# A graph layer pair on one core: the memset behind each gather made 128x320, and the wait at a group's head taken out

## The reference, cut to what matters

```
h = relu(layernorm(x))
x = x + segment_sum over edges of ( h[src] @ weight[etype] )          # 16 edge types, 64x64 each
h = relu(layernorm(x))
m = relu( concat(h[src], h[dst], edge_attr) @ W1 + b1 ) @ W2 + b2
x = x + segment_sum over edges of m, by dst
```

## Time and profile before

| | |
|---|---|
| median of three runs | 4952.87 us |
| profiled execution | 4951.48 us, of which the span is 4949.3 us |
| busy: PE / PEld / DVE / ACT / POOL | 55% / 31% / 30% / 12% / 69% |
| mean granted TensorE clock | 0.69 |
| gathers in the two loops | 1533 and 1661 |
| mean of one gather | 947 and 951 ns |

### The profile page before, as it was taken

How to read it: one execution, slowest core, us unless ns; L and a number is a source line. 1 busy time by engine, 2 the same in 40 slices (tenths; PEclk the granted TensorE clock), 3 DMA queues, 4 the chain that set the end, 5 groups by cost and what they waited for, 6 DMA issues and landing times.

```text
span 4949.3 us, 40507 instructions
## 1 busy us (share of the span) xinstructions
PE 2744.9 (55%) x10310; PEld 1528.5 (31%) x10310; DVE 1470.4 (30%) x2002; ACT 582.2 (12%) x1139; POOL 3439.7 (69%) x6536
## 2 busy tenths in 40 slices
PE   2656555565565655566655454555555554555555
PEld 1434333343343333333422222222222222222222
DVE  6323222222222222222233332333233232332333
ACT  3111111111111111111110000000000000000000
POOL 7567676676776776676756676777777767767676
PEclk8777777777777767776766666666666666666666
DMA  4111111111111111111111111111111111111111
GB/s 100 21 25 25 27 25 24 24 27 24 25 27 25 25 27 25 24 27 24 25 29 29 29 29 30 29 30 31 29 31 31 29 29 30 29 30 32 28 30 26
DMA packets 391188, 144.16 MB, mean 29 GB/s; under 512 B 321650, under 2 KB 337323, under 8 KB 391163
## 3 DMA queue, kind: packets, MB, share of 16 engines
q0 software_dynamic: 106304, 109.07, 11.5%
q1 hardware_dynamic: 282245, 34.18, 4.8%
q10 hardware_dynamic: 2614, 0.62, 0.1%
HBM read 129.03 MB, written 12.83 MB: 29 GB/s over the span
## 4 chain that ended last, share of the span: by engine, by line
POOL 34%; issue 23%; another core or an unknown queue 21%; PE 12%; DVE 6%; DMA 2%; DVEq 1%; ACT 1%; POOLq 0%; ACTq 0%; SPq 0%
POOL rows L710 31%; PE ps L1462 3%; PE ps L1379 2%; PE ps L1461 2%; POOL spacer L743 2%; PE ps L1466 1%; DVE z_slot L1230 1%; DVE slots L1219 1%; DVE q_blk L1243 1%; DMA rows<-p_table,idx 1%; DVEq L1234 1%; POOL spacer L763 1%; PE ps L1386 1%; DMA rows<-h_table,idx 1%
## 5 line engine op out<-in xcount | busy, mean ns | idle before, releaser
L710 POOL DMA_INDIRECT rows<-p_table,idx x1661 | 1580.3, 951 | 728.9 <-issue 510.2
L710 POOL DMA_INDIRECT rows<-h_table,idx x1533 | 1451.9, 947 | 695.9 <-issue 417.5
L1379 PE MATMUL ps<-onehot,rows 128*64 128x256 f32 x3328 | 742.2, 570 | 500.6 <-DMA rows<-h_table,idx 407.2
L1461 PE MATMUL ps<-w_attr,attr_t 64*128 64x512 f32 x416 | 368.0, 980 | 1087.4 <-DVE q_blk L1243 753.8
L1095 DVE TENSOR_TENSOR onehot<-key,ps 128x2048 f32<-128x2048 f32 x209 | 473.9, 2278 | 532.0 <-remote 344.6
L1379 PEld LDWEIGHTS ps<-onehot,rows 128*64 128x64 f32 x3328 | 364.5, 199 | 787.4 <-issue 693.2
L1219 DVE TENSOR_TENSOR slots<-ps,rows 128x512 f32<-128x512 f32 x208 | 143.8, 692 | 1263.0 <-remote 698.4
L1386 PE MATMUL ps<-w_types,slots 128*128 128x128 f32 x3328 | 464.2, 297 | 86.6 <-issue 85.3
L1386 PEld LDWEIGHTS ps<-w_types,slots 128*128 128x128 f32 x3328 | 430.6, 209 | 163.7 <-issue 157.8
L1461 PEld LDWEIGHTS ps<-w_attr,attr_t 64*128 64x128 f32 x416 | 87.8, 262 | 1125.2 <-issue 1124.8
L1462 PE MATMUL ps<-q_blk,onehot 128*128 128x512 f32 x416 | 405.9, 1077 | 0.0
(11 more groups left out here) (142 smaller groups left out, 1939.3 us busy)
## 6 DMA issues: line engine op xcount, KB each, us to landing
rows<-p_table,idx POOLq DMA_INDIRECT x1661
rows<-h_table,idx POOLq DMA_INDIRECT x1533
attr<-in_edge_attr_dram SPq DMA_DIRECT2D x52, 128.0 KB
q_win<-q_table SPq DMA_DIRECT2D x208, 32.0 KB
p_table<-pq_out SPq DMA_DIRECT2D x25, 120.0 KB
q_table<-pq_out SPq DMA_DIRECT2D x25, 120.0 KB
out_dram<-xs SPq DMA_DIRECT2D x25, 120.0 KB
xs<-in_x_dram SPq DMA_DIRECT2D x6, 480.0 KB, 6.3
```

The costliest lines, as they stand in the source:

```text
L710: pool.indirect_dma_start(rows[:, u, t, :], None, table, bass.IndirectOffsetOnAxis(ap=at, axis=0)).then_inc(s, 16)
L1379: last = pe.matmul(slot_ps[t % 2 * D:(t % 2 + 1) * D, b, t // 2, :], rows[:, u, t, :], onehot[:, b, t, :], start=True, stop=True)
L1461: pe.matmul(pre_ps[:, u % 2, :], attr_t[half, u // 2, :], w_attr[half].rearrange("k j d -> k (j d)"), start=True, stop=False)
```

## The change

The memset behind a gather writes 128 partitions by 320 columns in place of one cell. All of them write the same cells, so each waits for the one before it (`spaced`), which was issued one gather earlier. The wait for the group before at a group's head goes, in both loops. The other waits at the head stay. The counter `spaced` starts at 1 in place of 8.

```diff
-        spacer = sb("spacer", [1, T], fp32)
+        spacer = sb("spacer", [P, 5 * D], fp32)
...
+            def space(n):
+
+                wait_apart(pool, spaced, n + 1)
+                pool.memset(spacer[:], 0.0).then_inc(spaced, 1)
+
+            pool.sem_inc(spaced, 1)
...
-                pool.sem_inc(spaced, T)
-
                 def turn_of_rows(it, last=False):
                     for u in range(U):
-                        wait_apart(pool, spaced, T * ((it - 2) * U + u + 1))
...
                             gather(h_table, u, t, rows_in[u])
-                            pool.memset(spacer[:, t:t + 1], 0.0).then_inc(spaced, 1)
+                            space(((it - 2) * U + u) * T + t - (SKIP if last and u == U - 1 else 0))
...
                 def turn_of_groups(it, last=False):
                     for u in range(U):
-                        wait_apart(pool, spaced, T * ((NIT - 2 + it) * U + u + 1) - SKIP)
...
                             gather(p_table, u, j, rows_in[u])
-                            pool.memset(spacer[:, j:j + 1], 0.0).then_inc(spaced, 1)
+                            space(((NIT - 2 + it) * U + u) * T + j - (2 if last and u == U - 1 else 1) * SKIP)
```

## The result

The changed kernel takes 5087.93 us against 4952.51 for the kernel before on the same chip: ratio 1.027, interval 1.0242 to 1.0298. It is slower. (One of its four runs took 5245.97 us and is left out of the ratio.) Its profiled execution took 5075.26 us with a span of 5073.1, so 124 us more than the span before.

The account below looks back on a forecast made before the run. POOL's gathers were taken to set the pace, though not alone. Slower gathers less free heads' gains gave +306 us over 398 groups; with held heads between -6 and +279, +110 was taken on 4951: about 5060 us, range 4800 to 5260.

Parts of the forecast that it names:

- The memset is not hidden: Behind each gather in POOL's loops: the wide memset makes each gather come 0.19 us later, between 0 and 0.28; chance 0.42.
- The row's own 0.21: Before a gather's recorded start on POOL: about 0.21 us of its own, perhaps done only when the memset is through.
- The wait before each memset is hidden: Before each memset on POOL: waiting for the memset one gather back costs nothing, with some 0.2 us to spare.
- A free head gains 0.75 us: At the 269 group starts where POOL waits for no late engine: dropping wait and small memset saves 0.75 us each.
- The held heads: At 129 of 398 group starts POOL waits for another engine; they lose 312 us above a free head's 1.05.
- the head at 1033.01: A first-stage group start where POOL idles 3.66 us, 2.72 waiting and 0.73 issuing; TensorE was taken to be late.
- two fifths of the way: For the whole kernel: +110 us, taken between -6 (no head held any more) and +279 (releases as late as now).
- the pauses at the heads were caused by the pace of the gathers itself: At POOL's group heads: the stated alternative mechanism if the gather period is above 1.4 us while the time falls.
- the sum with no held head: Over 398 groups: +306 us less the 312 us of held heads, if the late engine catches up, totals -6.
- Hidden: Rival in POOL's loops: the memset fits into the 0.30 us pause, leaving the heads' gain, 4827 us; chance 0.33.
- partly hidden: Rival in POOL's loops: the memset adds 0.05 to 0.12 us a gather, time between 4900 and 5000; chance 0.15.
- Fully behind: Rival in POOL's loops: the memset adds 0.28 us a gather, about +400 us, 5350 us; chance 0.10.

Follow-up runs that it names:

- bare gathers: The kernel before without the loops' memsets and without the waits for them, the other waits at the heads kept: 5121.23 us, ratio 1.0212.

## Why the prediction came out

The sign and the size are right: 5060 forecast, 5087.93 measured, inside the range. Two errors that offset each other stand behind it, one of size and one of reason, and that they nearly cancel is luck.

- **The memset is not hidden.** Right, and under-sized. The forecast took 0.19 us a gather between bounds of 0 and 0.28; it is 0.243, so the period is 1.495 where 1.44 was forecast. The step that was low is "a little lower because the free small memset leaves it open that part of the 0.21 runs beside it": the one-cell memset fits into the pause because it is short; of the wide one's 0.38 us 0.243 is added. The row's own 0.21 was low too, as it took 0.30 for the memset from start to start; with the reported 0.38 and the 0.165 idle behind it the sum is 0.545, less 0.30. The Trainium skill, "Perfetto Trace Analysis", section "GPSIMD Engine Instruction", warns off reported spans on this engine. Here the reported duration counted, in the period of every size run: 0.95 + 0.22 + 0.17 at 128 columns, 0.95 + 0.38 + 0.17 at 320. The mis-sized term is worth 398 x 8 x 0.053 = 169 us.
- **The wait before each memset is hidden.** Right: 2.0 us over 3194 of them.
- **A free head gains 0.75 us.** Right in kind: heads look like the inside of a group. By the trace with 256 columns and the head's wait it is 0.79, by the steps before 0.80.
- **The held heads.** Here the reasoning failed, in two steps. The first is the reading of the head at 1033.01, "TensorE's timeline says who was late": the last matmul of that sum ended at 1029.02, before POOL's wait began at 1029.52, and it is the signal that came 3.2 us later. The second is "longer groups should cover more of them than they uncover". The forecast had two fifths of the way between a sum in which no head is held any more and one in which all hold, as if the delay of TensorE were a given length and the group a cover. All 129 went, and in the changed kernel the cover was not why: the delays themselves are gone, 4 of ScalarE's waits in place of 64, because the gathers come more slowly. The bare gathers show it from one side, where less work on POOL brought 197 held heads. A cover helps only where delays are left, as with 256 columns. The prediction had named this case, "the pauses at the heads were caused by the pace of the gathers itself", but only for a falling time. The price of the step: +110 took 116 us more than the sum with no held head, -6.
- **How they offset.** With the measured 0.243 the sum for no held heads is 398 x (8 x 0.243 - 0.75) - 312 = +163 us, and +124 was measured. The one error took 169 us off, the other put 116 on; 39 us are left over, of which the larger steps at the heads are 23.
- **The rivals.** Hidden and partly hidden fall with the period. "Fully behind" was near in the period (1.53 against 1.495) and far off in the time, 5350 us, for the same reason as above: it kept most of the held heads.

What stays open is why TensorE's signals come late. They do at a mean step of 1.44 us and less, and no longer at 1.495. It is not the transfers, which land on time, and not the bytes or the rows of a gather; packets, of which each gather has 32 whatever its size, and the gather as such were not told apart.

## What to carry to other kernels

Waiting time on the bounding engine that is put down to other engines can be that engine's own doing: before it is priced as a given, make the bounding engine slower in one run and look whether the others' idle stretches go. Where a stream of gathers is slowed, price the added step times its count against all of the waits that the stream causes, and look for the width where both are small; here it was 224 columns, 0.6% faster than before (the intervals of 192 and 256 columns overlap its own), while 320 columns pay 3194 x 0.077 = 246 us more to be rid of the last 63 us of delays. A short instruction that hides in a pause says nothing about a long one: here the step grew by the long one's reported time and the 0.165 us behind it, less the pause of 0.30. And before an engine is called late, compare the end of its work with the moment at which the one that waits for it was released.

## What was not expected of the hardware

- Gathers that follow one another at 1.25 us hold up TensorE's signals: one reached ScalarE 15.3 us after the matmul's end, and 64 waits at that step have no named releaser. With 256 columns, at 1.44 us, 66 of these waits are left; at a mean of 1.495 us there are 4. The gathers themselves land 2.1 us after their start at either pace.
- The mean rate counts: steps of 1.25 and 1.74 us in turn hold up nobody.
- The time that POOL spends on a gather hardly hangs on its size: 0.90 us for 64 rows, 0.95 for 128, and 0.94 for 128 rows of half the bytes.
